# Attention and expert tower: maxima run 16 items ahead, k and q are made a part earlier, and the order of transfers changes

## What is computed

```python
h = relu(grouped_conv(embedding[x]))                 # (2, 1024, 128)
x = layernorm(h)
q, k, v = (x @ W.T for W in (Wq, Wk, Wv))            # 8 heads of 64
attn = softmax(q @ k.T * 64 ** -0.5)                 # per batch and head: 1024 x 1024
h = h + (attn @ v) @ Wo.T + x
h = h + ffn(layernorm(h))                            # norm, linear, experts 128-512-128 with gelu, linear, gelu
```

## Time and profile before

| | us |
|---|---|
| runs (three) | 392.24, 392.33, 392.68 |
| median | 392.33 |
| the profiled execution | 392.45 |
| its span | 390.4 |
| TensorE busy, of the span | 379.4 |
| chain that ended last | TensorE 90%, VectorE 5%, ScalarE 2% |
| granted clock of TensorE, mean | 1.0 of full speed |

### The profile page before, as it was taken

One profiled execution on the slowest core, in us unless ns is written; L12 is line 12 of the kernel. 1 busy time (PEld: TensorE's weight loads), 2 busy tenths in 40 slices (PEclk: granted clock), 3 DMA queues, 4 the chain that ended last, 5 costly groups with the idle time before them and its releaser, 6 DMA issues.

```text
span 390.4 us, 6725 instructions
## 1 busy us (share of the span) xinstructions
PE 379.4 (97%) x2382; PEld 222.4 (57%) x2382; DVE 270.1 (69%) x476; ACT 273.3 (70%) x388; POOL 293.1 (75%) x145
## 2 busy tenths in 40 slices
PE   8999999999999999999999999999999998999996
PEld 7756545554464455445545544555447444489995
DVE  6998677777868786777768777868775664665222
ACT  3666656678958886896888688868972787337753
POOL 3080476969999999999999999999999597700021
PEclk9999999999999999999999999999999999999999
DMA  4001002101212021103111331241024105000001
GB/s 141 12 0 40 15 3 57 54 3 55 58 54 55 3 56 56 56 10 82 20 56 52 77 98 50 57 162 57 3 57 164 54 3 162 0 2 15 14 29 54
DMA packets 28228, 19.45 MB, mean 50 GB/s; under 512 B 21248, under 2 KB 23680, under 8 KB 28196
## 3 DMA queue, kind: packets, MB, share of 16 engines
q1 hardware_dynamic: 27620, 18.05, 16.7%
q10 hardware_dynamic: 576, 0.98, 0.8%
HBM read 17.72 MB, written 1.17 MB: 48 GB/s over the span
## 4 chain that ended last, share of the span: by engine, by line
PE 90%; DVE 5%; ACT 2%; issue 2%; DVEq 0%
PE psum L669 29%; PE psum L658 24%; PE psum L596 11%; PE psum L584 5%; PE psum L605 4%; PE psum L726 4%; PE psum L715 4%; PE psum L560 3%; PE psum L680 2%; PE psum L535 1%; PE psum L621 1%; PE psum L623 1%; PE psum L734 1%; ACT probs L855 1%; PE psum L509 1%
## 5 line engine op out<-in xcount | busy, mean ns | idle before, releaser
L1088 DVE TENSOR_REDUCE half_maxes<-psum 128x1 f32<-128x512 f32 x232 | 149.0, 684 | 36.6 <-PE psum L596 35.8
L855 ACT ACTIVATE probs<-psum 128x1024 f32<-128x1024 f32 x128 | 124.7, 1022 | 60.3 <-PE psum L658 59.8
L669 PE MATMUL psum<-probs,v_all 128*64 128x512 f32 x512 | 123.7, 604 | 0.0
L1305 POOL TENSOR_TENSOR sums<-sums,probs 128x1024 f32<-128x1024 f32 x31 | 74.5, 2402 | 3.4 <-ACT probs L855 3.4
L1305 POOL TENSOR_TENSOR odd_sum<-odd_sum,probs 128x1024 f32<-128x1024 f32 x31 | 74.4, 2400 | 0.0
L669 PEld LDWEIGHTS psum<-probs,v_all 128*64 128x64 f32 x512 | 31.2, 136 | 62.8 <-issue 44.3
L1305 POOL TENSOR_TENSOR sums<-probs 128x1024 f32<-128x1024 f32 x16 | 38.1, 2379 | 31.0 <-ACT probs L855 31.0
L1133 DVE TENSOR_SCALAR psum<-max_plane 128x512 f32<-128x512 f32 (+1 forms) x50 | 40.5, 822 | 28.4 <-ACT probs L855 26.6
L596 PE MATMUL psum<-k_round,q_round 64*128 64x512 f32 x256 | 57.0, 446 | 2.0 <-DVE half_maxes L1088 1.1
L596 PEld LDWEIGHTS psum<-k_round,q_round 64*128 64x128 f32 x256 | 24.0, 183 | 53.9 <-DVE half_maxes L1088 41.4
L658 PE MATMUL psum<-q_round,k_round 64*128 64x512 f32 x256 | 52.4, 404 | 2.2 <-DVE psum L1133 2.2
(11 more groups left out here) (123 smaller groups left out, 451.3 us busy)
## 6 DMA issues: line engine op xcount, KB each, us to landing
max_plane<-rows_scratch SPq DMA_DIRECT2D x16, 512.0 KB, 3.7
inv_sb<-inv_scratch SPq DMA_DIRECT2D x14, 256.0 KB, 4.0
max_rows_of<-maxes SPq DMA_DIRECT2D x128, 0.5 KB, 2.0
v_all<-in_fc SPq DMA_DIRECT2D x4, 512.0 KB, 5.8
fc_late<-in_fc SPq DMA_DIRECT2D x4, 512.0 KB, 5.6
out_h<-probs SPq DMA_DIRECT2D x8, 128.0 KB, 1.8
v_all<-in_w ACTq DMA_DIRECT2D x3, 256.0 KB, 3.6
woT<-in_wo SPq DMA_DIRECT2D x1, 256.0 KB, 3.6
```

The lines of the kernel that those rows point to most:

```text
L669: last = pe.matmul(out_bank[head_rows(h), :], v_all[:, s, kc, head_rows(h)], probs[unit(s, kc, half) % TILES][:, h, :], start=(kc == 0), s ...
L855: last = act.activation(probs[u % TILES][:, heads, :], source, ACT.Exp, scale=SCALE)
L1088: dve.reduce_max(half_maxes[:, h, qc, keys:keys + 1], slot[:, h, :], AX.X).then_inc(maxed, 1)
L1305: pool.tensor_tensor(chain[:, :, :], first[:, :, :], probs[kc][:, :, :], ALU.add).then_inc(own, 1)
```

## The change

Maxima: `FIRST_COUNTS` becomes two entries longer, so parts 5 and 6 of step 0 have three `max` items and the maxima run 16 ahead; the last ones are then in part 7 of step 6, and none are in step 7. k and q: those of step s + 2 are made in part 7 of step s; those of step 1 stay in part 1 of step 0. Unfilled units: of each full step only `(s, 1, 0)` stays so, behind q, and `(s, 0, 0)` is filled behind k. Fills for part 0 of a step are made in part 7 of the step before. In step 7 two more units are filled. SyncE: the two functions are cut in five, and the columns of `max_rows(s + 1, 0)` are issued between the denominators' transfer and the store of the reciprocals, and its plane ahead of the spread of the reciprocals. The other constants follow from these.

```diff
-LATE_PLANES = [(s, kc, 0) for s in range(STEPS) for kc in (0, 1)]
-BEHIND_K = [(0, 4, 0)] + [(s, 2, 0) for s in range(1, STEPS - 1)]
-BEHIND_Q = [(0, 5, 0)] + [(s, 3, 0) for s in range(1, STEPS - 1)]
-FIRST_PLANES = [(0, kc, 0) for kc in (2, 3, 6)] + [(0, kc, 1) for kc in (0, 1, 2, 3)]
-UNFILLED = LATE_PLANES + BEHIND_Q + FIRST_PLANES + [(STEPS - 1, 4, 0), (STEPS - 1, 5, 0)]
+BEHIND_K = [(0, 4, 0)] + [(s, 0, 0) for s in range(2, STEPS - 1)]
+BEHIND_Q = [(0, 5, 0)] + [(s, 1, 0) for s in range(2, STEPS - 1)]
+FIRST_PLANES = [(0, kc, 0) for kc in (0, 1, 2, 3, 6)] + [(0, kc, 1) for kc in (0, 1, 2, 3)] + [(1, kc, 0) for kc in (0, 1)]
+UNFILLED = BEHIND_Q + FIRST_PLANES + [(STEPS - 1, 4, 0), (STEPS - 1, 5, 0)]
...
-SCALAR_FILLED = [u for u in FILLED if u[0] < STEPS - 1]
+BESIDE_LAST_VALUES = [(STEPS - 1, kc, 0) for kc in (0, 1)]
+SCALAR_FILLED = [u for u in FILLED if u[0] < STEPS - 1 or u in BESIDE_LAST_VALUES]
...
-VECTOR_FILLED = [u for u in FILLED if u in HALVED or u[0] == STEPS - 1]
+VECTOR_FILLED = [u for u in FILLED if u in HALVED or u not in SCALAR_FILLED]
...
-    if part == (0 if s > 0 else 1) and s + 1 < STEPS:
-        items += [("k", s + 1), ("q", s + 1)]
+    if (s, part) == (0, 1):
+        items += [("k", 1), ("q", 1)]
+    if part == PARTS - 1 and s + 2 < STEPS:
+        items += [("k", s + 2), ("q", s + 2)]
...
-FIRST_COUNTS = (1, 2, 3, 3, 3)
+FIRST_COUNTS = (1, 2, 3, 3, 3, 3, 3)
...
-    following = units_of(s, part + 1) if part + 1 < PARTS else []
+    following = units_of(*divmod(turn + 1, PARTS)) if turn + 1 < STEPS * PARTS else []
...
-                max_rows(s, 1)
+                load_rows(s, 1)
+                spread_rows(s, 1)
                 if s > 0:
-                    spread(s - 1)
+                    spread_sums(s - 1)
                 if s + 1 < STEPS:
-                    max_rows(s + 1, 0)
+                    load_rows(s + 1, 0)
+                if s > 0:
+                    store_inverse(s - 1)
+                if s + 1 < STEPS:
+                    spread_rows(s + 1, 0)
+                if s > 0:
+                    spread_inverse(s - 1)
```

More of the change, by code:

```diff
@@ L430, in _, with spread_sums, store_inverse, spread_inverse @@
             sp.dma_start(woT[:, :, :], wo_in).then_inc(wo_loaded, 16)
-            def spread(s):
+            def spread_sums(s):
                 sp.wait_ge(den_copied, s + 1)
                 sp.dma_start(den_flat[:, :], den_sb[0:128:32, :]).then_inc(den_spread, 16)
+            def store_inverse(s):
                 sp.wait_ge(inverted, s + 1)
                 sp.dma_start(inv_dram[:, :], inv_flat[:, :]).then_inc(inv_stored, 16)
+            def spread_inverse(s):
                 sp.wait_ge(inv_stored, s * 16 + 16)
@@ L444, in spread, with load_rows @@
                                  .partition_broadcast(D).rearrange("p a n -> p (a n)")).then_inc(inv_loaded, 16)
-            def max_rows(v, half):
+            def load_rows(v, half):
                 i = 2 * v + half
@@ L459, in max_rows, with spread_rows @@
                                      maxes[:, h, qc:qc + 1].bitcast(F32)).then_inc(rows_loaded, 16)
+            def spread_rows(v, half):
+                i = 2 * v + half
                 sp.wait_ge(rows_loaded, ROW_COUNT * (i + 1))
@@ L476, in _ @@
             sp.wait_ge(pads_made, 1)
-            max_rows(0, 0)
+            load_rows(0, 0)
+            spread_rows(0, 0)
             early, late = list(EARLY_EXPERTS), list(LATE_EXPERTS)
             for s in range(STEPS):
-                max_rows(s, 1)
+                load_rows(s, 1)
+                spread_rows(s, 1)
                 if s > 0:
-                    spread(s - 1)
+                    spread_sums(s - 1)
                 if s + 1 < STEPS:
-                    max_rows(s + 1, 0)
+                    load_rows(s + 1, 0)
[5 more added lines that the diff above has]
+                    spread_inverse(s - 1)
                 if s == PAIRS:
```

## The result

The changed kernel takes **393.96 us** as the median of seven runs (393.93 to 394.11), against 392.36 for the kernel before on the same chips; the ratio is 1.0038, with a 95% interval of 1.0029 to 1.0048. It is slower by 0.4%. The prediction said 394.2 us.

The account below looks back on a forecast made before the run. TensorE, busy for 97% of the span, was taken as the bound. 4.05 - 1.26 - 0.95 = +1.84 us on a median of 392.33 gave 394.2 us; forecast's own range 393.3 to 394.9 (chance 0.64), overall range 391.2 to 395.8.

Parts of the forecast that it names:

- parts 5 and 6 of step 0: Parts given a third maximum while VectorE has a fill: +1.90 and +2.15 us, together +4.05 us, nothing given back later.
- steps 0, part 7, to 7: Steady steps with k and q moved and fewer unfilled units: 97.57 us before, 96.31 after, so -1.26 us.
- step 7 to the projection: Last step: two unfilled units become filled and two maxima have gone ahead, four pairs and a little, -0.95 us.
- the rest: Behind the last step's stretch up to the output projection nothing changes: 0 us.
- The fill in front of the second maximum: Step 0, parts 5 and 6: VectorE's fill waits for an exponential ahead of the second maximum; +1.90 and +2.15 us.
- k waits for one exponential: Part with k and q: k's wait grows from 0.22 to 0.45 us; part 7.44 to 7.21 us, six times, -1.38.
- rival B: Every pair pays: the six waits for k don't grow, 1.38 us more is won, 392.8 us; chance 0.13.
- Rival A: Step 0: third maximum finds its banks free, front costs 0.46 to 1.34 us, total 390.6 to 391.5 us; chance 0.16.
- the ring: Step 0: three banks hold the maxima; a part's third maximum needs the first half of its second reduced by VectorE.
- its upper bound: Step 0, parts 5 and 6 behaving as three-maxima parts without a fill: 5.05 for 4.38 twice, 1.34 us.
- The transfers: SyncE: columns and plane ahead of the reciprocals' transfers cost nothing; plane some 5 us to spare, reciprocals 2.9 us.
- More fills: Per step ScalarE gets 1.03 and 0.61 us more, VectorE 0.69; both stay under 36 us, GpSimd's 35.4 under 35.9.

Follow-up runs that it names:

- the last two experiments: Changed kernel with step 0's third maximum between the two weighings, 391.99 us; the same with parts 2 to 4 ordered maximum, unit, maximum, weighing, maximum, unit, weighing, 391.95 us.

## Why the prediction was right, step by step

The terms of the sum, from the same points of both timelines, with the profiled executions:

| step of the prediction | forecast | measured |
|---|---|---|
| parts 5 and 6 of step 0 (62.99 to 71.28; 63.03 to 75.35) | +4.05 | +4.03 |
| steps 0, part 7, to 7 (71.28 to 292.33; 75.35 to 295.01) | -1.26 | -1.39 |
| step 7 to the projection (4.40; 3.53) | -0.95 | -0.87 |
| the rest (296.73 to the end; 298.54 to the end) | 0 | -0.1 |
| sum | +1.84 | +1.7 |

The measured sum is that of the two spans. The medians differ by 1.60 us, since 1.84 us lie around the profiled span now, for 2.05. No two large errors cancel: no row is off by more than 0.13. The count of matmuls with the rows of maxima is 38, as forecast.

*The fill in front of the second maximum*: right in mechanism and size, part 5 to 0.00 us (6.28 for 4.38 + 1.90), part 6 to 0.02 (6.04 for 6.06). Two kernels show it, one that moves the fill within VectorE's queue and one that gives it to ScalarE.

*k waits for one exponential, so only one of the two pairs pays*: right. The wait grew from 0.22 to 0.46 us, the part lasts 7.21 as forecast, and a pair put back in the second unit costs nothing while one in the first costs 0.21. The count of pairs, rival B, is refuted.

*Rival A*, that the ring does not bite, is refuted by the same rows. But its upper bound was worked out wrong. The 1.34 took 5.05 for 4.38 twice, though part 6 was an ordinary part of 3.91; it should have been 0.67 + 1.14 = 1.81, and the sum -0.40, about 391.9 us instead of at most 391.5. That is what the two kernels without a fill in the way measured (391.81 and 391.87). The forecast did not use this bound.

One reason against rival A said too little as well. The ring does set the 5.05 us in this order. But the wait at the third maximum is not all that keeps such a part above the 4.61 us that I counted for it: where the third maximum waits for nobody it still lasts 4.94 to 5.23 in the last two experiments, by the second maximum's wait and by what is lost beside the weighings. For the sum it didn't matter, because I took steps from rows that had these losses in them.

*The transfers.* SyncE in step 4, then GpSimd:

```profile
206.37 0.63 SPq L437 DMA_DIRECT2D den_flat<-den_sb  x1
207.10 5.01 SPq L466 DMA_DIRECT2D max_rows_of<-maxes  x8
212.16 0.59 SPq L442 DMA_DIRECT2D inv_scratch<-inv_flat  x1
215.00 0.53 SPq L475 DMA_DIRECT2D rows_scratch<-max_rows_of  x1
216.61 0.32 SPq L480 DMA_DIRECT2D max_plane<-rows_scratch  x1
217.02 1.15 SPq L450 DMA_DIRECT2D inv_sb<-inv_scratch  x2
```

```profile
223.59 2.39 POOL L1336 TENSOR_TENSOR attn_out<-attn_out,inv_sb 128x1024 f32<-128x1024 f32 x1 [0.41 <-DMA inv_sb<-inv_scratch]
```

The columns do come first and the plane is issued at 216.61, 12.0 us behind the denominators' matmuls (204.62), near the 11 that I had worked out; it was 19.3 before. But the 2.9 us to spare for the reciprocals were not there: they are issued 12.4 us behind the denominators' matmuls and not 11.6, the second of their two transfers is issued 0.6 us behind the first, and it took 5.9 us instead of 4.0. That is 3.3 us more, and GpSimd waits for them 0.41 us. So this margin was misjudged, and that nothing was lost by it is in part luck: it is the only such wait among seven, and GpSimd catches up. That the new order costs nothing was right; that it is worth 18 us, since the fill behind k couldn't be there without it, I didn't say.

*More fills*: ScalarE has 30.25 us per step and VectorE 27.72, forecast 30.4 and 27.7; GpSimd has 35.34 of 35.94 and isn't the bound. The Trainium skill ("SBUF — State Buffer", section "Who interferes with whom") says that a tensor_scalar on VectorE can take the port pair that it shares with GpSimd. If these fills did, GpSimd's adds would have become longer; they last 2.39 us on average in the changed kernel (2387 and 2392 ns in the two largest groups of the page), not more than before, so no run here shows the rule at work.

The best version here is the changed kernel with the fill behind the third maximum, or without it: 391.8 to 391.9 us, 0.13% to 0.15% faster than the kernel before, which is at the edge of what can be told: the intervals end at 0.9994 and 0.9996.

## What to carry to other kernels

An engine that is busy 70% of the time, as VectorE is here, can still hold the bound engine, if one of its instructions that must wait stands ahead of one that is waited for: look at the order within its queue before its load. A matmul taken away is worth its time only if what comes next on TensorE doesn't wait for another engine anyway; find the wait behind it, and count from there. Work that is moved out of a stretch was also distance in time there: ask which transfer was hidden by it.

## What the runs showed of the hardware

Pairs of matmuls follow each other every 0.23 us here, a maximum behind the scores of a unit too (220.72, 220.95). Beside a weighing (128*64 in the rows, where the pairs are 64*128) TensorE loses 0.07 to 0.20 us: the first pair behind one is followed after 0.34 us, whether it is a maximum (68.61, 68.95 in the kernel with the third maximum between the weighings) or scores (295.01, 295.35), and a pair between two weighings after 0.43. The first pair behind a wait for VectorE is followed after 0.30 to 0.31 (69.99, 70.29 there; 70.69, 71.00 in the changed kernel). A handful of these in a part was as much as the wait that I had seen. What causes the loss no run here separates.

The transfers of the reciprocals (256 KB each) landed 3.5 to 4.5 us after their issue in the kernel before, with a median of 4.0, and 3.7 to 7.0 with a median of 5.2 in the changed kernel. There, in all but the last pair of them, the plane (512 KB) is issued 0.4 us ahead on the same queue. The two loads of 512 KB that follow in later steps are not needed for it: behind a plane the transfers took 4.9 to 6.2 us without such loads and 5.0 to 7.0 with them, and the last pair, with loads but without a plane, took 3.7 to 5.1.
